# Soft-MoE dispatch stage on Trainium2: column and row maxima turned between the two tiles of the second gather

## What is computed

```python
xn = _layernorm(x, ln_gamma, ln_beta)
x_unit = _l2norm(xn, axis=-1)
logits = jnp.einsum('bnd,des->bnes', x_unit * scale, mu_unit)
dispatch = jax.nn.softmax(logits, axis=1)                      # over the 64 tokens
combine = jax.nn.softmax(logits.reshape(B, N, E * S), axis=-1)  # over 256 slots
slot_in = jnp.einsum('bnd,bnes->besd', xn, dispatch)
h = gelu(jnp.einsum('besd,edh->besh', slot_in, w1) + b1)
slot_out = jnp.einsum('besh,ehd->besd', h, w2) + b2
out = jnp.einsum('besd,bnes->bnd', slot_out, combine)
```

## Time and profile before

| what | value |
|---|---|
| median of three runs | 507.67 us (506.4 to 509.29) |
| the profiled execution | 506.03 us, its span 504.2 us |
| PE busy | 461.2 us, 91% of the span |
| DVE, ACT, POOL busy | 413.8, 375.3 and 289.0 us |
| dispatch stage | about 298 to 428 us |
| mean granted TensorE clock | 0.993 of full speed |

### The profile page before, as it was taken

How to read it: one execution, slowest core, us unless ns; L and a number is a source line. 1 busy time by engine, 2 the same in 40 slices (tenths; PEclk the granted TensorE clock), 3 DMA queues, 4 the chain that set the end, 5 groups by cost and what they waited for, 6 DMA issues and landing times.

```text
span 504.2 us, 21722 instructions
## 1 busy us (share of the span) xinstructions
PE 461.2 (91%) x8732; PEld 316.9 (63%) x8732; DVE 413.8 (82%) x1118; ACT 375.3 (74%) x563; POOL 289.0 (57%) x380
## 2 busy tenths in 40 slices
PE   3999998999879999999998879999999997899995
PEld 1777776655446666666665556565655555788884
DVE  4788667879688898898887888898988865899995
ACT  3888866888888788788788558888888667655550
POOL 3444223874758768778765756789999842013000
PEclk9999998999999999999999899999999999999999
DMA  6377549630001101111111111223323234277664
GB/s 198 84 181 186 147 124 243 175 108 1 1 25 28 46 27 35 38 27 37 36 27 38 33 43 44 110 88 109 97 100 125 79 121 154 68 223 210 188 181 119
DMA packets 53311, 49.22 MB, mean 98 GB/s; under 512 B 14192, under 2 KB 40944, under 8 KB 53232
## 3 DMA queue, kind: packets, MB, share of 16 engines
q1 hardware_dynamic: 53232, 48.13, 32.8%
HBM read 30.81 MB, written 17.04 MB: 95 GB/s over the span
## 4 chain that ended last, share of the span: by engine, by line
PE 34%; DVE 17%; POOL 15%; issue 5%; ACT 3%; DMA 1%; POOLq 0%; DVEq 0%; SPq 0%; ACTq 0%
DVE c_mx L635 10%; PE ps L1638 6%; PE ps L1557 6%; PE ps L863 3%; POOL v_or_front L1045 3%; PE ps L1461 3%; PE ps L965 3%; PE ps L834 2%; DVE copies_or_layer L626 2%; PE ps L1194 2%; POOL e_inv_root L1074 2%; PE ps L896 2%; POOL e_scaled L1356 2%; POOL e_inv_root L1059 2%; POOL k_or_hidden L1364 2%
## 5 line engine op out<-in xcount | busy, mean ns | idle before, releaser
L635 DVE TENSOR_REDUCE c_mx<-ps 128x16 f32<-128x1024 f32 x64 | 78.0, 1219 | 20.3 <-PE ps L834 20.3
L572 POOL TENSOR_TENSOR copies_or_layer<-k_or_hidden,w_mask 128x512 bf16<-128x512 f32 x80 | 83.5, 1070 | 2.6 <-DVE c_work L666 2.6
L737 ACT ACTIVATE c_work<-ps 128x2048 f32<-128x2048 f32 x32 | 59.9, 1872 | 23.8 <-PE ps L863 23.6
L1530 ACT ACTIVATE copies_or_layer<-k_or_hidden 32x512 f32 (+1 forms) x64 | 40.2, 628 | 24.8 <-PE ps L1557 24.2
L1356 POOL TENSOR_TENSOR e_scaled<-e_raw,e_rden 128x512 f32<-128x512 f32 x16 | 20.8, 1298 | 45.2 <-DMA e_rden<-dispatch_inverses 45.2
L1543 DVE TENSOR_TENSOR o_slot_out<-ps,w_b 128x512 f32<-128x512 f32 x64 | 41.2, 686 | 6.1 <-PE ps L1557 5.6
L1407 ACT ACTIVATE e_slot_in<-ps 128x1024 f32<-128x1024 f32 x30 | 30.7, 1022 | 17.2 <-PE ps L1461 17.2
L747 ACT ACTIVATE c_q_bd<-x_all,w_mask 128x512 f32<-128x512 f32 x64 | 42.7, 719 | 0.0
L592 POOL COPY c_v_bd<-v_or_front 64x512 f32<-64x512 f32 x32 | 21.6, 676 | 30.7 <-PE ps L883 29.4
L1461 PE MATMUL ps<-copies_or_layer,v_or_front 64*128 64x256 f32 x256 | 36.0, 400 | 3.5 <-ACT e_slot_in L1407 3.1
L1638 PE MATMUL ps<-o_slot_out,ctx_sb 128*64 128x129 f32 x512 | 36.8, 282 | 1.4 <-DMA ctx_sb<-combine_scratch 0.9
(11 more groups left out here) (165 smaller groups left out, 1173.7 us busy)
## 6 DMA issues: line engine op xcount, KB each, us to landing
x_all<-x_scratch SPq DMA_DIRECT2D x64, 128.0 KB, 3.2
combine_scratch<-v_or_front SPq DMA_DIRECT2D x16, 512.0 KB, 2.7
ctx_sb<-combine_scratch SPq DMA_DIRECT2D x16, 512.0 KB, 3.3
x_sb<-in_x SPq DMA_DIRECT2D x16, 256.0 KB, 3.2
x_scratch<-a_x SPq DMA_DIRECT2D x16, 256.0 KB, 2.4
ctx_sb<-in_ctx SPq DMA_DIRECT2D x16, 256.0 KB, 3.5
e_rden<-dispatch_inverses SPq DMA_DIRECT2D x64, 64.0 KB, 2.1
out<-o_y SPq DMA_DIRECT2D x32, 128.0 KB, 3.0
```

What stands on the lines that cost most here:

```text
L572: ins = nc.gpsimd.tensor_tensor(k_bd[:, c.m2, s, :], k32[:, c.v, :], w["mask8"][:, s:s + 1].to_broadcast([P, TOK]), ALU.mult)
L635: nc.vector.reduce_max(mx[:, c.m2, :, p], ps[:, SCORE:SCORE + 2, :].rearrange("p a (h m) -> p (a h) m", m=N), AX_X).then_inc(mx_sb.sem, 1)
L737: nc.scalar.activation(prob[:, h, :], ps[:, 0:4, :].rearrange("p a b -> p (a b)"), ACT.Exp, scale=float(HD) ** -0.5).then_inc(p_sb.sem, 1)
L1530: ins = self.nc.scalar.activation(self.h_bd[at, c.m2, :, :, e % 2, :].rearrange("p s g k -> p g s k"), self.hidden[at, :, bass.ts(c.v, SC ...
```

## The change

Three calls move. `turn_tokens` takes a list of tiles and runs in two parts: tiles 0 and 1 ahead of the second gather, tiles 2 and 3 behind it. `gather` takes the chunk whose maxima are turned between its tiles a = 0 and a = 1. On DVE, `invert` goes from ahead of `maxima` to behind it. No instruction is added or taken away.

```diff
-    def turn_tokens(self, pe, c):
+    def turn_tokens(self, pe, c, tiles=range(PC)):
         if not c:
             return
-        pe.wait_ge(self.xu_sb.sem, self.xu_sb.at(c))
-        if c.plus(-1): pe.wait_ge(self.xuT_sb.sem, self.xuT_sb.at(c.plus(-1)))
-        for p in range(PC):
+        if tiles[0] == 0:
+            pe.wait_ge(self.xu_sb.sem, self.xu_sb.at(c))
+            if c.plus(-1): pe.wait_ge(self.xuT_sb.sem, self.xuT_sb.at(c.plus(-1)))
+        for p in tiles:
             ins = self.nc.tensor.transpose(self.ps[:, self.xuT_bank(c), p * P:(p + 1) * P], self.xu[:, c.m2, p, :], self.w["ident"][:])
-        ins.then_inc(self.xuT_ps.sem, 1)
+        if p == PC - 1: ins.then_inc(self.xuT_ps.sem, 1)
...
                     self.copies(dve, t.plus(1))
+                    self.maxima(dve, t.plus(1))
                     c = t.plus(-2)
                     if c and c.plus(3): invert(dve, c)
-                    self.maxima(dve, t.plus(1))
                     self.gathered(dve, t.plus(5))
...
-            def gather(c, h):
+            def gather(c, h, between=None):
...
                 for a in range(2):
+                    if a and between: self.turn_maxima(pe, between)
                     for r in range(2):
...
                 self.logits(pe, t.plus(1))
-                gather(t.plus(0), 1)
-                self.turn_maxima(pe, t.plus(1))
-                self.turn_tokens(pe, t.plus(2))
+                self.turn_tokens(pe, t.plus(2), range(0, 2))
+                gather(t.plus(0), 1, t.plus(1))
+                self.turn_tokens(pe, t.plus(2), range(2, 4))
                 self.shifts(pe, t.plus(1))
```

## The result

The changed kernel takes 516.05 us (median of six runs, 515.12 to 518.32); the kernel before took 506.52 in six runs, the three of the section on the time before among them. The ratio is 1.0192, with a 95% interval of 1.0159 to 1.0225. So it is slower, by 9.5 us where 6.9 were forecast.

A forecast was written before the change was run, and what follows sets the result against it. PE was taken to bound the kernel, with POOL just as long from step 4 on. 14 x 0.48 + 0.14 = 6.9 us, added to the median 507.67, gave 514.6 us, range 509.0 to 517.7.

The forecast's parts named there:

- Joint A: Second gather waits for ACT's copy of the first; two token transposes ahead fill 0.19 us idle and cost 0.11.
- The maxima's start: Between the second gather's halves PE idles 0.17 us for DVE's row maximum; moving the inverse brings it 0.12 forward.
- Rival B: Between the gather's halves: maxima ready in time, no added wait; gather 0.32 us late, 512.2 us; chance 0.14.
- The second half of the gather: On PE behind the maxima: takes 0.53 us, half of 1.06; the gather ends 0.49 us later, taken as 0.48.
- Rival C: Breaking the second gather costs PE a 0.10 us surplus twice; steps 0.58 longer, 516.1 us; chance 0.10.
- Joint B: Expert matmuls (L1480) wait for ACT's copy of the second gather; they start 0.48 us later, PE idles about 0.5.
- Rival D: At the expert matmuls: shifts, not ACT's copy, release them; not slower, 506.3 to 507.7 us; chance 0.10.
- The step: Dispatch steps, between starts of L1194, lengthen from 8.115 to 8.60 us.
- Step 12: Dispatch step whose ACT copy was already 0.34 us late behind POOL; longer steps absorb that, so it costs 0.14.
- The late inverse: DVE's inverses come 2.4 us later; slack to POOL is 4.1 us, so nothing; SP's transfers slip harmlessly too.
- What sets the step: In the dispatch stage PE sets the 8.115 us step; from step 4 on POOL is just as long.

The follow-up runs named there:

- e3: Kernel before with only the tokens split: tiles 0 and 1 ahead of the second gather, 2 and 3 behind the maxima; 504.8 us, ratio 0.9974.
- e5: Changed kernel with DVE's inverse back ahead of the maxima; 516.54 us, ratio 1.0232 to the kernel before.
- e6: Changed kernel with the column maxima taken over 32 of the 64 tokens only; 515.58 us (one run).
- e4: Kernel before with tokens 0 and 1, not the maxima, between the second gather's halves; 514.15 us, ratio 1.016.
- e7: Changed kernel with ACT's copy of the second gather cut to half its elements from chunk 2 on; 508.49 us (one run).
- e1: Kernel before with only DVE's inverse moved behind the maxima; 509.27 us, ratio 1.0075.
- c1: Changed kernel measured again without further edits; 517.55 us, ratio 1.0203 to the kernel before.

## Why the prediction was right, and where its sizes were off

The direction, the place and the mechanism held: slower, inside the range, by a wait for DVE between the halves and by the late copy behind it. By its steps:

- **Joint A and the tokens.** Forecast: 0.11 us. Measured: 0 (2.36 against 2.35, and e3). The logits were taken to end at the idle's start, 1.10 after their own start; transposes behind them start after 0.93.
- **The maxima's start.** Forecast: 3.16 us after the first gather (321.33 - 318.17). Measured: 3.18. The middle value of 0.12 for the inverse was right within 0.02 (e5: 0.10). The end of the gather's first half came out right, 2.99 us after the first gather, only because two errors cancel: the 0.11 too much at joint A and 0.10 too little for the half. Rival B, the maxima ready in time, is out: PE waits about 0.19 for them, though in the changed profile that wait has no label of its own; e6 shows a second bound 0.1 us below.
- **The second half of the gather.** Forecast: half of 1.06, 0.53. Measured: 0.64. This is the term that was mis-sized. A burst costs about 0.20 of its own (e4), and half a burst is not half the time. The sign given for C, halves that take well over 1.06 together, is there: 0.63 + 0.64. Rival C had the mechanism with 0.10 from the rows of L1194; the doubled cost came on top of the wait, with the first half's share hidden in it, as C's case against said. Forecast and C are thus both in the result.
- **Joint B.** Forecast: the copy releases the expert matmuls, everything late at the gather's end arrives, about 0.5 of idle. Measured: 0.62 late, all of it arrived, 0.42 idle, and e7 gives it back. Rival D is out.
- **The step.** Forecast: 8.60. Measured: 8.73. Step 12 was forecast at 0.14 extra and took 0.30 (8.73 against 8.43), which is its older delay of 0.32 (8.43 - 8.115) taken off 0.62. Steps 0 to 13 gave 8.30, and with 0.38 for step 14 that is 8.7 us against 6.9.
- **The late inverse.** Forecast: nothing. This step failed. The slack on the way to POOL was worked out and holds, as the steps of e1 show. But "both feed things a step or more away" was said of SyncE's other transfers without following them into the last steps, where two loads of 512 KB wait in the same queue. Cost: 1.3 to 3.7 us of tail beyond step 14's share in the two profiles of the changed kernel, 2.7 in e1, where it stands alone.
- **What sets the step.** The prediction said PE. e3 fills PE's idle at joint A and leaves less work behind the gather, and the step stays 8.115; the chain through ACT's two copies has its part in it from the start.
- **Luck.** 516.05 lies only 1.5 us above the forecast of 514.6, but the kernel before took 506.52 here, 1.15 less than the 507.67 that the forecast was added to. As a difference, 9.5 us, the result is beyond C's 8.4 too, and the tail had no term in the prediction.

## What to carry to other kernels

Moving work into the middle of a burst of matmuls makes the burst end later by the wait for that work's data, its own time, and one more burst's fixed cost (0.20 us here for a 64-row gather of 1.06), less what of that cost the wait hides. Here all of it went into the step, since another engine waits for the end of the burst. A transfer order that runs on one queue has to be followed to the end of the stage: a small step that is late by 2 us in its queue can push large loads into the moment at which another engine enters the next stage. And a steady loop in which every engine is 85 to 98% busy may still be set by a chain through two of them: here shortening ACT's copy helped (e7), while filling PE's idle did not (e3).

## What the runs showed of the hardware that was not expected

- PE stops for 0.3 to 3.3 us on entering the second layer, after the same 123 matmuls each time, with no releaser in the profile. How long goes with how busy the DMA engines are at that time (share 0.98 over four microseconds: 3.34 us; 0.54: 0.88 us; 0.10: 0.31 us). It ends 1.2 to 1.5 us after a 16 KB packet on the DMA queue that the profile calls "instruction", in all fourteen profiles.
- In e1, after an idle of 3.34 us, the mean granted clock was 0.57 from 431 to 434 us, so for most of that time it was at the lower of its two levels (1.2 GHz). In the changed kernel, after 2.78, it was 0.81 and then 0.62 over three microseconds each. In the kernel before, after 0.88, it stayed at 1.00, and so it did in c1 after 1.89.
- Four fp32 transposes took 0.61 us and two 0.37; a gather of two tiles 1.06 and of one 0.63.
